# Recommendation tower on one core: the first chunk's gathers, constants and pair tiles in another order and on other engines

## The chip, the cores and the metric

One core of one Trainium2 chip. The metric is the device time of one execution in microseconds (us), lower is better. Before the change: 1389.95 us, the median of 3 runs (1387.94 to 1392.07).

## The reference, cut to what matters

For 1024 samples, 39 tables give one row of 16 numbers each, `e[b, f, d]`. Three layers follow, each a sum over all pairs of an original field and a field of the layer before, and then a small network:

```
e  = stack([tbl_f[ids[:, f]] for f in range(39)], axis=1)      # 1024 x 39 x 16
x1 = einsum('hjk,bjd,bkd->bhd', W0, e, e)  + b0                # 128 x 16 per sample
x2 = einsum('hjk,bjd,bkd->bhd', W1, e, x1) + b1
x3 = einsum('hjk,bjd,bkd->bhd', W2, e, x2) + b2
z  = concat([x1.sum(d), x2.sum(d), x3.sum(d), dense_ctx])
y  = relu(relu(z @ W_top1 + b_top1) @ W_top2 + b_top2) @ W_top3
```

## The kernel before, in words

The samples are worked in 8 chunks of 128. A step function of each engine is called for c = -1, 0, ..., 9; step c does layer 1 (`x2`) of chunk c in 16 slices d, and around it layer 0 of the next half chunk, the gathers of the chunks after, and the third layer and the network of the chunks before. In step -1 there is no layer 1: it is the start-up, and the change is in it and in the code ahead of it.

**Getting a chunk in.** GpSimd copies the chunk's indices into `idx` (L402, later L415) and issues 39 indirect DMAs (`gather`, L396 to L399), one a table, into `e_in`. ScalarE copies `e_in` into `e_mid`, the first 58 columns of `e_both`: the 39 fields, and 19 of them once more behind (L514, L515). TensorE transposes it (L900), ScalarE copies the result to `x0_t` (L555), where a field is a partition; four copies q = 0 to 3, two a half chunk. Ahead of the first gather GpSimd also makes the identity matrix (L403, L405) and clears the rest of `e_both` (L407).

**Layer 0** works on products of a field and a shifted field. A half chunk (1024 columns) has 7 pair tiles (`PAIR_TILES`); a chunk's tiles are numbered 0 to 13, so tile 7, the eighth, is the first of the second half. A tile holds 3 shifts of 39 rows, 117 partitions (the seventh 2 shifts, 78 partitions). For each, SyncE issues one DMA a shift from `x0_t` to the tile's slot (`pair_tile`, L312), 156 KB each. `x0_rep` holds the unshifted fields three times over (`rep`, L319; for the very first half ScalarE issues these three, L596). Then a tile passes through four operations: the product in place (VectorE L720 for tiles 0 to 7 of chunk 0, GpSimd L429 for all others), its upper part `pairs_hi` (ScalarE L532), its low part `pairs_lo` (VectorE L725 or GpSimd L440), and 6 matmuls into `l0_ps` (L843 to L845). The first seven tiles of chunk 0 have 4 slots, two of them in `x2_r`; all later ones have 2. `pairs_hi` and `pairs_lo` have 2 buffers.

**Order around the change.** Each engine works in the order in which its program is written; semaphores are counters. In step -1, slice d = 8 to 15 handles tile d - 8 of chunk 0 on VectorE (`first_pairs`: product and low part of the same tile, with the wait for ScalarE between them) and on ScalarE (`pair_upper`). SyncE waits before tile 4, 5 and 6 for the low part of tile 0, 1 and 2 (L306); it reloads `x0_rep` once all 7 products are made (`rep(c + 1, 1)`, L317), and loads tile 7 behind that. TensorE multiplies tile 0 to 6 in step -1; then ScalarE makes `x1_hi` (L503), VectorE `x1_lo` and a partial sum (L690, L699), and layer 1 of chunk 0 begins. There, in each slice d, TensorE does ten groups of matmuls (L938 to L940) into a ring of 4 banks; ScalarE (L626) and VectorE (L777 to L785) scale and add them. TensorE's queue takes tile 7 behind group 3 and group 5 of slice 0, tile 8 in slice 1, and so on, and waits there for the tile's low part. ScalarE makes `pairs_hi` of tile 7 ahead of its first group, and that of tiles 8 to 13 ahead of group 7 of slices 0 to 5.

GpSimd's order: 39 gathers of chunk 0; in step -1 the 24 first gathers of chunk 1 (slices 6 to 15, three of them in slice 15); in slices 0 to 4 of step 0 the product of tile 8 + d, three gathers, the low part of tile 8 + d.

```
        def tile_made(c, d, layer1, following):
            if d < PAIR_TILES - 1:
                return (c, PAIR_TILES + 1 + d) if layer1 else None
            if d < D // 2:
                return None
            return (c + 1, d - D // 2) if following else None
```

Of the kernel before, what the change touches and what calls it, by code (L numbers as in the profile page):

```python
# [4 lines left out]
FIELDS, D, H = 39, 16, 128  # L5
# [4 lines left out]
def build_tower(nc, dense_ctx, ids, tables, W_top1, b_top1, W_top2, b_top2, W_top3, W0, b0, W1, b1, W2, b2, out):  # L10
# [90 lines left out]
    Z0_AT = {1: (7, 7), 0: (15, 8)}  # L101

    MID, MOVE_MID, HI_MID, G_EARLY = 3, 2, 7, 8
    MADE_MID, LO_MID = 1, 7
    BLOCK_FIRST, BLOCK_SLOTS = 7, 4

    GATHERS = (3, 3, 3, 3, 3, 0, 6, 5, 1, 1, 2, 2, 1, 2, 1, 3)
# [9 lines left out]
    with ctx:  # L117
# [163 lines left out]
        def _(sp):  # L281
# [18 lines left out]
            def step(c, odd, layer1, following, previous, mlp, gathers):  # L300
# [68 lines left out]
                if following:  # L369
                    if layer1:  # L370
                        rep(c + 1, 0)
                    else:
                        after(sp, x0t_ready, 2)
                    for i in range(PAIR_TILES):
                        pair_tile(c + 1, i)
                        if layer1 and i in X2_WRITES:
                            x2_write(c, X2_WRITES[i])
                    rep(c + 1, 1)
                    pair_tile(c + 1, PAIR_TILES)
# [14 lines left out]
        @block.gpsimd  # L394
        def _(pool):
            def gather(chunk, f):  # L396
                nc.gpsimd.indirect_dma_start(  # L397
                    e_in[:, f, :], None, tables[f], bass.IndirectOffsetOnAxis(ap=idx[:, f:f + 1], axis=0)
                ).then_inc(gathered, 16)  # L399

            pool.wait_ge(ids_in, 16)
            nc.gpsimd.tensor_copy(idx[:, :], ids_sb[:, 0, :]).then_inc(idx_ready, 1)  # L402
            nc.gpsimd.memset(ident[:, :], 0.0).then_inc(zeroed, 1)  # L403
            pool.wait_ge(zeroed, 1)
            nc.gpsimd.affine_select(out=ident[:, :], in_=ident[:, :], compare_op=ALU.not_equal, fill=1.0, base=0,  # L405
                                    pattern=[[-1, P]], channel_multiplier=1).then_inc(consts_made, 1)
            nc.gpsimd.memset(e_both[:, WRAPPED:WRAPPED + FIELDS, :], 0.0).then_inc(e_cleared, 1)  # L407
            pool.wait_ge(idx_ready, 1)
            for f in range(FIELDS):
                gather(0, f)  # L410
# [1 line left out]
            def step(c, odd, layer1, following, previous, mlp, gathers):  # L412
# [6 lines left out]
                def multiply_pairs(chunk, i):  # L419

                    half, t = TILE[i]
                    n = TILES * chunk + i
                    rows = ROWS_OF[t]
                    products, loaded, count = pair_slot(chunk, i)
                    if isinstance(chunk, int) and chunk == 0 and i == PAIR_TILES + 1:
                        pool.wait_ge(pair_made, n)
                    after(pool, rep_in, 16 * PER_TILE * (2 * chunk + half + 1))
                    after(pool, loaded, count)
                    nc.gpsimd.tensor_tensor(products[0:rows, :], x0_rep[0:rows, :], products[0:rows, :],  # L429
                                            ALU.mult).then_inc(pair_made, 1)  # L430

                def lower_pairs(chunk, i):

                    n = TILES * chunk + i
                    rows = ROWS_OF[TILE[i][1]]
                    if isinstance(chunk, int) and chunk == 0 and i == PAIR_TILES + 1:
                        pool.wait_ge(pair_lo, n)
                    after(pool, pair_hi, n + 1)
                    after(pool, pair_used, n - 1)
                    nc.gpsimd.tensor_tensor(pairs_lo[0:rows, i % 2, :], pair_slot(chunk, i)[0][0:rows, :],  # L440
                                            pairs_hi[0:rows, i % 2, :].bitcast(f32),
                                            ALU.subtract).then_inc(pair_lo, 1)
# [11 lines left out]
                        own[:, :].unsqueeze(1).to_broadcast(shape), ALU.mult).then_inc(block_made, 1)  # L454

                for d in range(D):
                    made = tile_made(c, d, layer1, following) if layer1 else None
                    if made:
                        multiply_pairs(*made)
                    if previous and BLOCK_FIRST <= d < BLOCK_FIRST + G_GROUPS // 2:  # L460
                        for i in range(2):
                            make_block(2 * (d - BLOCK_FIRST) + i)
# [5 lines left out]
                    if gathers and d >= INDEX_SLICE:  # L468
                        for f in range(sum(GATHERS[INDEX_SLICE:d]), sum(GATHERS[INDEX_SLICE:d + 1])):
                            gather(c + 2, f)  # L470
                    if made:
                        lower_pairs(*made)

            steps(pool, step)
# [2 lines left out]
        def _(act):  # L477
# [20 lines left out]
            def step(c, odd, layer1, following, previous, mlp, gathers):  # L498
# [7 lines left out]
                def move_x0(d):  # L506

                    if following and d == MOVE_SLICE:
# [2 lines left out]
                        after(act, e_cur_ready, c + 1)  # L511
                        if layer1:
                            act.wait_ge(dve_unit, summed(c, CUR_FROM, 0))
                        nc.scalar.activation(e_mid[:, 0:FIELDS, :], e_in[:, :, :], ACT.Copy)  # L514
                        nc.scalar.activation(e_mid[:, FIELDS:WRAPPED, :], e_in[:, 0:WRAPPED - FIELDS, :],  # L515
                                             ACT.Copy).then_inc(e_mid_ready, 1)
                    if layer1 and d == COPY_SLICE:
                        after(act, dve_unit, summed(c, 0, 0))
# [68 lines left out]
                for d in range(D):  # L587
                    if not layer1:
# [4 lines left out]
                        if following and d == X0T_SLICES[0] + 1:  # L593
                            act.wait_ge(x0t_ready, 2)
                            for n in range(PER_TILE):
                                act.dma_start(x0_rep[n * FIELDS:(n + 1) * FIELDS, :],  # L596
                                              x0_t[0:FIELDS, 0:HALF]).then_inc(rep_in, 16)
                        for half, chunk in halves(c, layer1, following):
                            if d == X1_HI_AT[half][0]:
                                x1_half(chunk, half)  # L600
# [37 lines left out]
        @block.vector  # L638
        def _(dve):

            dve.wait_ge(w0_in, 16)
            nc.vector.tensor_copy(v_raw[:, 0:FIELDS], w0_raw[:, 0:FIELDS * FIELDS:FIELDS + 1])
            for s in range(1, SHIFTS):
# [41 lines left out]
            def step(c, odd, layer1, following, previous, mlp, gathers):  # L685
# [20 lines left out]

                def first_pairs(d, g):

                    made = tile_made(c, d, layer1, following)
                    made_at, lo_at = (8, 9) if d == D - 1 else (MADE_MID, LO_MID)  # L710
                    if made and g in (made_at, lo_at):
                        chunk, i = made
                        n = TILES * chunk + i
                        half, t = TILE[i]
                        rows = ROWS_OF[t]
                        products, loaded, count = pair_slot(chunk, i)
                        if g == made_at:
                            after(dve, rep_in, 16 * PER_TILE * (2 * chunk + half + 1))
                            after(dve, loaded, count)
                            nc.vector.tensor_tensor(products[0:rows, :], x0_rep[0:rows, :], products[0:rows, :],  # L720
                                                    ALU.mult).then_inc(pair_made, 1)
                        else:
                            after(dve, pair_hi, n + 1)
                            after(dve, pair_used, n - 1)
                            nc.vector.tensor_tensor(pairs_lo[0:rows, i % 2, :], products[0:rows, :],  # L725
                                                    pairs_hi[0:rows, i % 2, :].bitcast(f32),
                                                    ALU.subtract).then_inc(pair_lo, 1)

                def sum_terms(e, part):

# [16 lines left out]
                def side_work(d, g):  # L747
                    for half, chunk in halves(c, layer1, following):
                        if (d, g) == X1_LO_AT[half]:
                            x1_lower(chunk, half)  # L750
                        if (d, g) == Z0_AT[half]:
                            z0_half(chunk, half, odd)
                    if not layer1:
                        first_pairs(d, g)

                for d in range(D):
# [218 lines left out]
```

## Time and profile before

| | us |
|---|---|
| median of 3 runs | 1389.95 |
| lowest, highest | 1387.94, 1392.07 |
| the profiled execution's own time | 1388.79 |
| its span in the trace | 1386.9 |
| mean granted TensorE clock | 0.969 |
| TensorE busy | 1277.4 (92%) |
| VectorE, ScalarE, GpSimd busy | 1082.3, 1042.6, 893.5 |

How to read it: times in the trace count from the span's start; 1.9 us of the execution's time lie outside the span. A row of a timeline says when an instruction started, how long it took, its engine, its source line, out<-in, and in brackets how long its engine stood idle before it and what ended that. A letter q behind the engine is its queue issuing a DMA. TensorE's busy time is that of matmuls alone; the granted clock is a share of 2.4 GHz, so 0.5 is 1.2 GHz.

### The profile page before, as it was taken

Reading aid. Unit: us, or ns where it says so; the run is one execution under the profiler, and the core shown is the slowest. Engines: PE = TensorE matmul, PEld = TensorE weight load, DVE = VectorE, ACT = ScalarE, POOL = GpSimd, SP = SyncE. Lnnn points to the kernel's source line nnn. Section 1 sums busy time; section 2 is a strip of 40 time slices with the busy share of each in tenths; the row PEclk is TensorE's granted clock in tenths of the full one; section 3 lists DMA queues with packets and bytes.
Section 4 is the critical chain, followed back from the end, with each engine's and each line's share of the span. In section 5 each row is a group of like instructions: output and inputs, shape, how many; then the busy total and the mean of one; then the engine's idle time right before and its main releaser. Section 6 shows DMA issues by size and latency. Waiting matters only on the chain.

```text
span 1386.9 us, 23238 instructions
## 1 busy us (share of the span) xinstructions
PE 1277.4 (92%) x6029; PEld 1041.8 (75%) x6029; DVE 1082.3 (78%) x2681; ACT 1042.6 (75%) x3356; POOL 893.5 (64%) x663
## 2 busy tenths in 40 slices
PE   3179999999999999999999999999999999999986
PEld 3147777777888787887878777887878788887775
DVE  3068999988877988789877988789877988779940
ACT  2228888878877888788867888688877888688842
POOL 6658676877776687667867597667876266441111
PEclk8559999999999999999999999999999999999998
DMA  6243223413232223303242223313233123310010
GB/s 221 42 115 68 46 72 80 106 30 83 67 97 46 48 63 85 92 21 80 62 108 50 52 63 74 92 33 72 56 90 79 32 68 83 89 32 9 18 39 0
DMA packets 71116, 92.39 MB, mean 67 GB/s; under 512 B 31776, under 2 KB 53792, under 8 KB 69696
## 3 DMA queue, kind: packets, MB, share of 16 engines
q1 hardware_dynamic: 60836, 87.75, 24.4%
q0 software_dynamic: 9984, 2.58, 2.1%
q8 instruction: 53, 0.87, 0.3%
q14 instruction: 87, 0.71, 0.2%
q10 hardware_dynamic: 156, 0.48, 0.1%
HBM read 21.03 MB, written 10.95 MB: 23 GB/s over the span
## 4 chain that ended last, share of the span: by engine, by line
PE 70%; POOL 8%; DVE 7%; issue 6%; DMA 3%; ACT 2%; SPq 2%; ACTq 0%; DVEq 0%; POOLq 0%
PE ring L938 16%; PE ring L940 15%; PE ring L939 15%; PE side L856 5%; POOL e_in L397 4%; PE side L915 4%; PE l_ps L843 4%; PE l_ps L845 3%; PE l_ps L844 3%; DVE terms L785 3%; DVE x_s L741 2%; PE side L871 2%; POOL pairs L429 2%; DMA x_rep<-x_t 2%; POOL pairs_lo L440 2%
## 5 line engine op out<-in xcount | busy, mean ns | idle before, releaser
L626 ACT ACTIVATE terms<-ring,e_both 128x128 f32<-128x128 f32 x2944 | 836.3, 399 | 221.9 <-PE ring L940 219.9
L938 PE MATMUL ring<-w_hi,x_hi 128*128 128x512 f32 (+1 forms) x1280 | 544.8, 426 | 31.4 <-DVE terms L785 27.7
L785 DVE SCALAR_TENSOR_TENSOR terms<-ring,e_both,terms 128x128 f32<-128x128 f32 x1792 | 508.2, 344 | 62.7 <-PE ring L940 58.0
L940 PE MATMUL ring<-w_hi,x_lo 128*128 128x512 f32 (+1 forms) x1280 | 499.7, 390 | 0.0
L939 PE MATMUL ring<-w_lo,x_hi 128*128 128x512 f32 (+1 forms) x1280 | 498.2, 389 | 0.0
L741 DVE TENSOR_REDUCE x_s<-terms 128x32 f32<-128x800 f32 x512 | 488.9, 976 | 0.1
L440 POOL TENSOR_TENSOR pairs_lo<-pairs,pairs_hi 117x1024 fp32r<-117x1024 f32 (+1 forms) x104 | 250.2, 2406 | 191.6 <-ACT pairs_hi L532 190.6
L397 POOL DMA_INDIRECT e_in<-in_tbl,idx x312 | 306.1, 981 | 88.3 <-issue 79.4
L938 PEld LDWEIGHTS ring<-w_hi,x_hi 128*128 128x128 f32 x1280 | 242.8, 190 | 103.0 <-DVE terms L785 42.1
L429 POOL TENSOR_TENSOR pairs<-x_rep,pairs 117x1024 f32<-117x1024 f32 (+1 forms) x104 | 250.3, 2407 | 92.3 <-DMA pairs<-x_t 89.3
L939 PEld LDWEIGHTS ring<-w_lo,x_hi 128*128 128x128 f32 x1280 | 243.4, 190 | 49.2
L940 PEld LDWEIGHTS ring<-w_hi,x_lo 128*128 128x128 f32 x1280 | 241.5, 189 | 50.8
L451 POOL TENSOR_TENSOR blocks<-xb,own 128x312 f32<-128x312 f32 x128 | 90.5, 728 | 87.7 <-PE side L915 87.7
L777 DVE SCALAR_TENSOR_TENSOR terms<-ring,e_both,b_rows 128x128 f32<-128x128 f32 x128 | 44.8, 350 | 119.7 <-PE ring L940 119.5
L532 ACT ACTIVATE pairs_hi<-pairs 117x1024 fp32r<-117x1024 f32 (+1 forms) x109 | 119.7, 1099 | 19.1 <-DVE pairs L720 18.2
L843 PE MATMUL l_ps<-pairs_hi,v_hi 117*128 117x512 f32 (+1 forms) x224 | 96.4, 430 | 21.8 <-DVE pairs_lo L725 16.9
L856 PEld LDWEIGHTS side<-g_t,w_t 128*128 128x128 f32 x624 | 88.0, 190 | 12.1 <-ACT g_t L539 2.4
L845 PE MATMUL l_ps<-pairs_lo,v_hi 117*128 117x512 f32 (+1 forms) x224 | 91.8, 410 | 0.0
L844 PE MATMUL l_ps<-pairs_hi,v_lo 117*128 117x512 f32 (+1 forms) x224 | 91.7, 409 | 0.0
L856 PE MATMUL side<-g_t,w_t 128*128 128x128 f32 x624 | 89.3, 274 | 1.4 <-ACT g_t L539 1.4
L915 PE MATMUL side<-blocks,x_r 128*128 128x320 f32 x256 | 89.0, 434 | 0.9 <-issue 0.3
L843 PEld LDWEIGHTS l_ps<-pairs_hi,v_hi 117*128 117x128 f32 (+1 forms) x224 | 44.0, 196 | 39.8 <-DVE pairs_lo L725 21.2
(65 smaller groups left out, 610.6 us busy)
## 6 DMA issues: line engine op xcount, KB each, us to landing
pairs<-x_t SPq DMA_DIRECT2D x312, 156.0 KB
x_scratch<-x_s SPq DMA_DIRECT2D x32, 256.0 KB, 2.2
x_r<-x_scratch SPq DMA_DIRECT2D x8, 1024.0 KB, 6.0
x_rep<-x_t SPq DMA_DIRECT2D x45, 156.0 KB
g_t<-in_L_rec_W SPq DMA_DIRECT2D x2, 2496.0 KB, 9.5
e_in<-in_tbl,idx POOLq DMA_INDIRECT x312
x_scratch<-e_both SPq DMA_DIRECT2D x8, 312.0 KB, 7.2
xb<-x_scratch SPq DMA_DIRECT2D x8, 312.0 KB, 3.9
```

Of the source, the lines that this page charges most:

```text
L397: nc.gpsimd.indirect_dma_start(e_in[:, f, :], None, tables[f], bass.IndirectOffsetOnAxis(ap=idx[:, f:f + 1], axis=0)).then_inc(gathered, 16)
L429: nc.gpsimd.tensor_tensor(products[0:rows, :], x0_rep[0:rows, :], products[0:rows, :], ALU.mult).then_inc(pair_made, 1)
L440: nc.gpsimd.tensor_tensor(pairs_lo[0:rows, i % 2, :], pair_slot(chunk, i)[0][0:rows, :], pairs_hi[0:rows, i % 2, :].bitcast(f32), ALU.subt ...
L626: last = nc.scalar.activation(term(d, ACT_BEFORE[d][g] + i), twos(ring[:, (GROUPS * d + g) % RING, i * H:(i + 1) * H]), ACT.Copy, scale=sc ...
L741: last = nc.vector.tensor_reduce(twos(x2_s[:, d % X2_SLOTS, h]), terms[:, d % 2, a, 0:TERMS[d], :].rearrange("p a t b -> p a b t"), AX.X, ...
L785: nc.vector.scalar_tensor_tensor(out=acc, in0=y, scalar=scale_of(j, d), in1=acc, op0=ALU.mult, op1=ALU.add).then_inc(dve_unit, 1)
L843: nc.tensor.matmul(acc, v_hi[0:rows, t, :], p_hi, start=(t == 0), stop=False)
L856: last = nc.tensor.matmul(side[:, 0, 0:P], w2_t[:, j * H:(j + 1) * H], g_t[:, j, :], start=(j == 0), stop=(j == FIELDS - 1))
L915: nc.tensor.matmul(side[:, r % 2, 0:SAMPLES_PER_G * GCOLS], x2_r[:, r, :], blocks[:, r % BLOCK_SLOTS, :, :].rearrange("p b j -> p (b j)"), ...
L938: nc.tensor.matmul(acc, x1_hi[:, x], w1_hi[:, w], start=True, stop=False)
L939: nc.tensor.matmul(acc, x1_hi[:, x], w1_lo[:, w], start=False, stop=False)
L940: nc.tensor.matmul(acc, x1_lo[:, x], w1_hi[:, w], start=False, stop=True).then_inc(y_group, 1)
```

## The change

Five edits, all in what runs before layer 1 of chunk 0:

- GpSimd makes the identity matrix first and then waits for the indices; the clearing of `e_both` goes to VectorE, as its first instruction.
- The gathers of chunk 0 write `e_mid` itself; the copy L514 falls away for it, and L515 reads `e_mid`.
- The three loads of tile 1 are issued by ScalarE, behind its three of `x0_rep`, and no more by SyncE.
- VectorE makes the product of tile i + 1 before the low part of tile i.
- Tile 7 of chunk 0 is multiplied and lowered by GpSimd, ahead of the last three gathers of its step -1.

```
-    MADE_MID, LO_MID = 1, 7
+    FIRST_MADE_AT, FIRST_LO_AT, FIRST_BY_ACT = 1, 3, 1
...
                     for i in range(PAIR_TILES):
+                        if not layer1 and i == FIRST_BY_ACT:
+                            continue
                         pair_tile(c + 1, i)
...
             def gather(chunk, f):
+                dst = e_mid if isinstance(chunk, int) and chunk == 0 else e_in
                 nc.gpsimd.indirect_dma_start(
-                    e_in[:, f, :], None, tables[f], bass.IndirectOffsetOnAxis(ap=idx[:, f:f + 1], axis=0)
+                    dst[:, f, :], None, tables[f], bass.IndirectOffsetOnAxis(ap=idx[:, f:f + 1], axis=0)
                 ).then_inc(gathered, 16)
-            pool.wait_ge(ids_in, 16)
-            nc.gpsimd.tensor_copy(idx[:, :], ids_sb[:, 0, :]).then_inc(idx_ready, 1)
             nc.gpsimd.memset(ident[:, :], 0.0).then_inc(zeroed, 1)
             pool.wait_ge(zeroed, 1)
...
-            nc.gpsimd.memset(e_both[:, WRAPPED:WRAPPED + FIELDS, :], 0.0).then_inc(e_cleared, 1)
+            pool.wait_ge(ids_in, 16)
+            nc.gpsimd.tensor_copy(idx[:, :], ids_sb[:, 0, :]).then_inc(idx_ready, 1)
...
                 for d in range(D):
-                    made = tile_made(c, d, layer1, following) if layer1 else None
+                    made = tile_made(c, d, layer1, following) if layer1 or d == D - 1 else None
                     if made:
                         multiply_pairs(*made)
+                        if not layer1:
+                            lower_pairs(*made)
...
-                    if made:
+                    if made and layer1:
                         lower_pairs(*made)
...
-                        nc.scalar.activation(e_mid[:, 0:FIELDS, :], e_in[:, :, :], ACT.Copy)
-                        nc.scalar.activation(e_mid[:, FIELDS:WRAPPED, :], e_in[:, 0:WRAPPED - FIELDS, :],
+                        if layer1:
+                            nc.scalar.activation(e_mid[:, 0:FIELDS, :], e_in[:, :, :], ACT.Copy)
+                        came_in = e_in if layer1 else e_mid
+                        nc.scalar.activation(e_mid[:, FIELDS:WRAPPED, :], came_in[:, 0:WRAPPED - FIELDS, :],
                                              ACT.Copy).then_inc(e_mid_ready, 1)
...
+                            products, loaded, _ = pair_slot(0, FIRST_BY_ACT)
+                            for n in range(PER_TILE):
+                                s = PER_TILE * FIRST_BY_ACT + n
+                                act.dma_start(products[n * FIELDS:(n + 1) * FIELDS, :],
+                                              x0_t[s:s + FIELDS, 0:HALF]).then_inc(loaded, 16)
...
+            nc.vector.memset(e_both[:, WRAPPED:WRAPPED + FIELDS, :], 0.0).then_inc(e_cleared, 1)
             dve.wait_ge(w0_in, 16)
...
                 def first_pairs(d, g):
-                    made = tile_made(c, d, layer1, following)
-                    made_at, lo_at = (8, 9) if d == D - 1 else (MADE_MID, LO_MID)
...
+                    if g == FIRST_MADE_AT and tile_made(c, d, layer1, following) and d < D - 1:
+                        chunk, i = tile_made(c, d, layer1, following)
...
+                        after(dve, rep_in, 16 * PER_TILE)
+                        after(dve, loaded, count)
+                        nc.vector.tensor_tensor(products[0:rows, :], x0_rep[0:rows, :], products[0:rows, :],
+                                                ALU.mult).then_inc(pair_made, 1)
+                    if g == FIRST_LO_AT and tile_made(c, d - 1, layer1, following):
+                        chunk, i = tile_made(c, d - 1, layer1, following)
...
+                        after(dve, pair_hi, i + 1)
+                        after(dve, pair_used, i - 1)
+                        nc.vector.tensor_tensor(pairs_lo[0:rows, i % 2, :], pair_slot(chunk, i)[0][0:rows, :],
+                                                pairs_hi[0:rows, i % 2, :].bitcast(f32),
+                                                ALU.subtract).then_inc(pair_lo, 1)
```

## Rows read from the trace of the kernel before

**Rows 1.** Windows, layer 1 of chunk 0, one a slice: length, busy (x) per engine, clock, DMA

```profile
core 0: us, PE busy (x) PEld busy (x) DVE busy (x) ACT busy (x) POOL busy (x), PEclk, DMA share, GB/s
104.80:113.25 8.45, 8.38 (x37) 6.67 (x37) 5.57 (x21) 7.36 (x26) 7.67 (x6) 1.00 0.25 60
113.25:121.70 8.45, 8.45 (x38) 6.60 (x37) 7.83 (x21) 7.28 (x24) 7.66 (x6) 1.00 0.27 62
```

**Rows 2.** Chain of work that ended last, start to first loads: start, us, what

```profile
51.50 0.94 POOL e_in L397
...
52.75 2.34 DMA e_in<-in_tbl,idx
55.20 0.72 ACT e_both L514
...
61.50 7.95 DMA x_rep<-x_t
```

**Rows 3.** Timeline of GpSimd: start, us, what, idle before

```profile
3.48 0.21 POOL L402 COPY idx<-ids_sb 128x39 int32<-128x39 int32 x1 [3.03 <-DMA ids_sb<-in_ids]
...
5.10 1.15 POOL L397 DMA_INDIRECT e_in<-in_tbl,idx  x1 [0.17 <-issue]
...
90.62 1.97 POOL L397 DMA_INDIRECT e_in<-in_tbl,idx  x1 [0.30 <-issue]
92.89 0.94 POOL L397 DMA_INDIRECT e_in<-in_tbl,idx  x1 [0.30 <-issue]
104.71 2.41 POOL L429 TENSOR_TENSOR pairs<-x_rep,pairs 117x1024 f32<-117x1024 f32 x1 [10.87 <-DMA pairs<-x_t]
...
110.78 2.42 POOL L440 TENSOR_TENSOR pairs_lo<-pairs,pairs_hi 117x1024 fp32r<-117x1024 f32 x1
113.15 2.40 POOL L429 TENSOR_TENSOR pairs<-x_rep,pairs 117x1024 f32<-117x1024 f32 x1
```

**Rows 4.** Timeline of SyncE's queue: DMA issues merged (x is their count)

```profile
59.01 9.69 SPq L312 DMA_DIRECT2D pairs<-x_t  x6
68.74 7.40 SPq L312 DMA_DIRECT2D x_r<-x_t  x6
76.24 6.16 SPq L312 DMA_DIRECT2D pairs<-x_t  x6
82.50 1.54 SPq L312 DMA_DIRECT2D x_r<-x_t  x2
91.84 2.33 SPq L319 DMA_DIRECT2D x_rep<-x_t  x3
```

**Rows 5.** Windows while the loads of step -1 run, columns as in rows 1

```profile
62.90:69.50 6.60, 0.00 (x0) 0.00 (x0) 0.03 (x1) 1.07 (x2) 4.83 (x6) 0.50 0.58 132
...
76.20:84.00 7.80, 6.19 (x13) 3.98 (x14) 5.55 (x6) 2.11 (x2) 6.28 (x6) 0.50 0.58 146
...
87.70:91.80 4.10, 3.52 (x9) 2.25 (x8) 2.94 (x3) 1.06 (x1) 3.49 (x3) 0.50 0.05 4
```

**Rows 6.** Timeline of VectorE: first and last of the seven tiles, tile 7

```profile
69.47 1.23 DVE L720 TENSOR_TENSOR pairs<-x_rep,pairs 117x1024 f32<-117x1024 f32 x1 [45.01 <-DMA x_rep<-x_t]
71.82 1.25 DVE L725 TENSOR_TENSOR pairs_lo<-pairs,pairs_hi 117x1024 fp32r<-117x1024 f32 x1 [1.12 <-ACT pairs_hi L532]
73.00 1.21 DVE L720 TENSOR_TENSOR pairs<-x_rep,pairs 117x1024 f32<-117x1024 f32 x1
...
90.56 1.21 DVE L720 TENSOR_TENSOR x_r<-x_rep,x_r 78x1024 f32<-78x1024 f32 x1
...
101.15 1.22 DVE L720 TENSOR_TENSOR pairs<-x_rep,pairs 117x1024 f32<-117x1024 f32 x1 [0.42 <-DMA pairs<-x_t]
```

**Rows 7.** Timeline of ScalarE: the second copy of e_both, pairs_hi of tile 7

```profile
55.83 0.44 ACT L515 ACTIVATE e_both<-e_in 128x304 f32<-128x304 f32 x1
...
102.41 1.06 ACT L532 ACTIVATE pairs_hi<-pairs 117x1024 fp32r<-117x1024 f32 x1 [4.13 <-DVE pairs L720]
```

**Rows 8.** Timeline of TensorE: start of layer 1, tiles 7 and 8

```profile
99.75 0.76 PE L938 MATMUL ring<-w_hi,x_hi 128*128 128x512 f32 x1 [2.62 <-DVE x_lo L690]
...
104.87 0.47 PE L843 MATMUL l_ps<-pairs_hi,v_hi 117*128 117x512 f32 x1 [0.44 <-DVE pairs_lo L725]
...
113.25 0.50 PE L843 MATMUL l_ps<-pairs_hi,v_hi 117*128 117x512 f32 x1
```

**Rows 9.** Windows around a stall of TensorE in chunk 1, columns as in rows 1

```profile
277.40:280.90 3.50, 1.19 (x5) 1.02 (x6) 3.14 (x7) 0.15 (x1) 3.50 (x2) 0.99 0.02 2
280.90:284.30 3.40, 3.40 (x10) 2.62 (x9) 0.00 (x0) 2.46 (x9) 2.94 (x3) 0.50 0.38 96
```

More of the change, by code:

```diff
@@ L424, in multiply_pairs @@
                     products, loaded, count = pair_slot(chunk, i)
-                    if isinstance(chunk, int) and chunk == 0 and i == PAIR_TILES + 1:
+                    if isinstance(chunk, int) and chunk == 0 and i == PAIR_TILES:
                         pool.wait_ge(pair_made, n)
@@ L435, in lower_pairs @@
                     rows = ROWS_OF[TILE[i][1]]
-                    if isinstance(chunk, int) and chunk == 0 and i == PAIR_TILES + 1:
+                    if isinstance(chunk, int) and chunk == 0 and i == PAIR_TILES:
                         pool.wait_ge(pair_lo, n)
@@ L707, in first_pairs @@
                 def first_pairs(d, g):
-                    made = tile_made(c, d, layer1, following)
-                    made_at, lo_at = (8, 9) if d == D - 1 else (MADE_MID, LO_MID)
[L711 to L715, printed above, removed]
-                        products, loaded, count = pair_slot(chunk, i)
[L717 to L727, printed above, removed]
@@ new lines, in first_pairs @@
+                    if g == FIRST_MADE_AT and tile_made(c, d, layer1, following) and d < D - 1:
+                        chunk, i = tile_made(c, d, layer1, following)
+                        rows = ROWS_OF[TILE[i][1]]
+                        products, loaded, count = pair_slot(chunk, i)
+                        after(dve, rep_in, 16 * PER_TILE)
+                        after(dve, loaded, count)
+                        nc.vector.tensor_tensor(products[0:rows, :], x0_rep[0:rows, :], products[0:rows, :],
+                                                ALU.mult).then_inc(pair_made, 1)
@@ new lines, in first_pairs @@
+                    if g == FIRST_LO_AT and tile_made(c, d - 1, layer1, following):
+                        chunk, i = tile_made(c, d - 1, layer1, following)
+                        rows = ROWS_OF[TILE[i][1]]
+                        after(dve, pair_hi, i + 1)
[3 more added lines that the diff above has]
+                                                ALU.subtract).then_inc(pair_lo, 1)
@@ L752, in side_work @@
                             z0_half(chunk, half, odd)
-                    if not layer1:
+                    if following and not layer1:
                         first_pairs(d, g)
```

## The prediction

> **What bounds the kernel now.** I read the windows first. In layer 1 of chunk 0 TensorE is busy 8.38 and 8.45 of 8.45 us a slice [rows 1]; whatever delays the start of this stage is added to the end, since nothing later is idle enough to take it back. So the question is only when a few early marks fall. The chain of waits says what makes them: 39 gathers, one a 1.25 us, a landing, two copies, a transposition, then the load of `x0_rep`, 7.95 us [rows 2]. After that the chain goes from tile to tile. I therefore follow three marks: S, the first load out of `x0_t`, at 59.0 [rows 4]; M, the product of tile 6, at 90.56 [rows 6]; and L, the end of the low part of tile 8, at 113.2 [rows 3]. L matters because GpSimd goes straight from it to the next product [rows 3]: its slice of product, three gathers and low part lasts 113.15 - 104.71 = 8.44 us, TensorE's 113.25 - 104.87 = 8.38 [rows 8], and TensorE takes up tile 8 at 113.25, 0.05 after L. For the first slices of chunk 0 GpSimd is as much the bound as TensorE, and it has no gap in which to catch up. The shift of L is the change of the whole time.
>
> **S.** The index copy ends at 3.69, the first gather starts at 5.10 [rows 3]; between them lie only the constants. With these first, the gather follows after the 0.17 that stands before it today: 3.86, 1.24 us earlier. The identity fits into the 3.03 us in which GpSimd waits for the indices. The clearing costs VectorE nothing: it idles until its weights arrive at the start, and if that cover were gone it would be 0.6 us. The gathers keep their 1.25 us, also into `e_mid`: same rows, same sizes. Of the two copies, from 55.20 to 56.27, one of 0.44 stays [rows 2, 7]: 0.63 less. S moves by 1.87, to 57.1.
>
> **From S to M: the loads.** VectorE's new order takes out its wait for ScalarE, 1.12 of a 3.53 us cycle [rows 6]: two operations at 1.18, 2.35 us a tile. If nothing else held, M would fall 13.0 after the first product (two products, a low part, then 4 cycles of 2.35), which starts 10.45 after S: 57.1 + 10.45 + 13.0 = 80.5. But the loads don't come so fast. 23 transfers of 156 KB (3 of `x0_rep`, 20 of tiles) start at S, and traffic falls to 4 GB/s from 87.7 on [rows 5], 28.7 us later: some 1.2 us each if 1.5 are latency (my estimate). The rate is 132 GB/s while both queues issue and 146 with SyncE's alone [rows 5]: a second issuer moved no more. So ScalarE's issuing of tile 1 frees SyncE's queue, not the transfers. Tile 5 lands at about 86.1 today: the last two transfers were issued 0.77 apart [rows 4] and end at 87.7. That is S + 27.1.
>
> In-order work adds something. Tile 1 used to follow tile 0 in SyncE's queue; now tile 2 does, and tile 1 shares with it from ScalarE's. At S + 10.45 some 7.5 transfers are through, 6 of them `x0_rep` and tile 0; tiles 1 and 2 have 4.5 left and end together at S + 15.8 (bounds: S + 14 as today, where VectorE found tile 1 there at 73.00; S + 19.5 if it ends last of the 15). VectorE now stands at the product of tile 1 while the low part of tile 0 could be made, and SyncE waits for that low part before tile 4: S + 15.8 + 2.4 = S + 18.2, against S + 17.2 today [rows 4]. Of this microsecond I take half, since the engines still have tile 3 to move: tile 5 lands at S + 27.6, 84.7. Behind its product comes the low part of tile 4, and then M: 84.7 + 2.4 = 87.1, 3.4 earlier than before.
>
> **From M to L: tile 7.** Its loads stay behind M: SyncE issues at M + 1.28 [rows 4], six transfers, landed at M + 10.5 (VectorE starts at 101.15 [rows 6]). Today VectorE and ScalarE then need 3.6, and GpSimd, which is idle for 10.87 us, starts tile 8 at M + 14.15, when that has landed [rows 3]. Now GpSimd does the work itself:
>
> - product at M + 10.6, 2.41 us [rows 3], to 13.1;
> - `pairs_hi`, 1.06 [rows 7], to 14.2; low part 2.41, to 16.65;
> - three gathers that used to lie in its idle time, 3.66 (107.12 to 110.78 [rows 3]), to 20.3: the moved instructions count in full, as they are ahead of tile 8;
> - tile 8: product 2.41, gathers 3.66, low part 2.42: M + 28.8.
>
> Today L is M + 22.64. So GpSimd pays 6.15 for a start 3.4 earlier: L = 87.1 + 28.8 = 115.9 against 113.2, **2.7 us later**.
>
> TensorE's side is hidden under this. It takes tile 5 only after M + 2.4 and tiles 5 and 6 back to back, so `x1_hi` comes 1.4 later after M than now and layer 1 at M + 10.6 (today 9.2 [rows 8]). Four groups at 1.2 GHz end by M + 15.7, before tile 7 is ready at 16.65; it then needs 8.4 to tile 8, M + 25.0, and waits 3.8. ScalarE stands in that stretch at group 7 for the product of tile 8 (M + 22.7): a new wait, and the ring's banks behind it stop TensorE for some 2.4 us, inside the same 3.8. VectorE's denser work stretches more gathers to 1.97 instead of 0.94 (today some of those beside its products are [rows 3]); 21 of them still end before tile 7 has landed.
>
> **Sum.** 1.87 (S) + 1.55 (loads and VectorE) - 6.15 (GpSimd) = 2.7 slower: 1388.8 + 2.7 = 1391.5 by the profiled execution, whose time is 1.16 under the median. Against the median: 1392.6. A difference under 0.3% (4.2 us) can't be told from none, so this is "no change that can be told".
>
> **Rivals.**
>
> 1. **Issue was the bound, not the transfers.** SyncE's 20 issues last 25.0 us, 1.25 each, though the last two took 0.77 each [rows 4]; read literally, three fewer bring the later tiles 3.75 earlier: tile 5 at S + 23.4, M at 82.9, L at 111.7: 1.5 faster, 1388.4. With no load late, M is 80.5 and L 109.3: 3.9 faster, 1386.0. Against it: the equal rates of rows 5. The Trainium skill (DMA: Bandwidth & Descriptors, "Issuing engines are not separate DMA queues") also holds that issuing from several engines saves the issuing time alone; by it the sum stays as it is, and the rates agree. 0.17.
> 2. **Slower: tile 1 lands last.** If the two queues share less evenly, tile 1 comes with the fifteenth transfer, S + 19.5. Low part of tile 0 at S + 21.9; then SyncE issues tile 4, tile 5 comes some 3 us behind it and lands near S + 31, its product, tile 4's low part, then M at S + 33.5, 90.6: nothing gained there, L at 119.4, 6.2 slower, 1396.2. It decides from S + 17.5 on, where L passes 4.2 later. For it: `x0_rep`, issued by ScalarE beside SyncE's loads, took 7.95 us to land [rows 2]. 0.14.
> 3. **The clock falls.** In chunk 1 TensorE was busy 1.19 of 3.5 us and then had a granted clock of 0.5 (1.2 GHz) for 3.4 us [rows 9]. A stall like that ahead of L costs half of the next 3.4 us, 1.7: 4.4 slower, 1394.4. Here 2.4 and 1.4 us of waiting lie close together, so it can be. The Trainium skill (TensorE: Matmul & The Clock Gate, "Part 1: The HAM clock gate") has the clock follow recent activity, down after idleness and up after work; rows 9 agree. 0.12.
> 4. **GpSimd's chain is not the bound.** Should it find slack that I don't see, layer 1's start counts: 87.1 + 10.6 = 97.7 against 99.75, 2.0 faster, 1388.0. Against it: rows 3 show no idle time behind 104.71. 0.07.
>
> My forecast itself has 0.5. The range 1386.0 to 1396.5 reaches from the second price of rival 1 to rival 2. Chances: faster by over 0.3% 0.09 (only gains that no row supports), within 0.68 (forecast, rivals 1 and 4, part of the unknown rest), slower by over 0.3% 0.23 (rivals 2, 3 in the main).
>
> **What would show it.** In the trace after: first gather at 3.9; one copy of 0.44 and S at 57.1; VectorE's products of tiles 2 to 6 each waiting for `DMA pairs<-x_t`, M near 87; GpSimd's product of tile 7 near 98, three gathers before tile 8, L near 116; TensorE's matmul of tile 8 waiting for `pairs_lo`, some 1 to 4 us. Slices of 8.4 behind it, and a span 2 to 3 us longer. It is wrong if products follow one another without waits for DMA (rival 1), if VectorE's second product waits over 8 us (rival 2), or if the clock reads 0.5 behind L (rival 3). If L falls before 113 the whole argument on GpSimd fails.

## The result, and the profile after

| | before | after |
|---|---|---|
| median of 12 runs | 1389.97 us (1387.94 to 1392.07) | 1397.3 us (1391.91 to 1399.3) |
| ratio, 95% interval | | 1.0048 [1.0035, 1.006] |
| profiled execution, its span | 1388.8, 1386.9 | 1397.21, 1395.4 |
| S, first load out of `x0_t` | 59.01 | 57.35 |
| M, product of tile 6 | 90.56 | 88.80 |
| L, end of the low part of tile 8 | 113.20 | 117.49 |
| `pairs_hi` of tile 9 | 116.97 | 122.80 |

The changed kernel is 0.48% slower, outside the range. The runs after are also less alike: 7.4 us from the fastest to the slowest against 4.1, the fastest (1391.91) with a mean granted clock of 0.978, the slowest (1399.3) with 0.971. Four of the five sets of runs below were taken while every kernel, the one before too, took 37 to 52 us more, so kernels are compared within their set alone, and of their traces only distances between marks are used.

GpSimd's timeline of the changed kernel (start, us, what, idle before):

```profile
3.46 0.21 POOL L409 COPY idx<-ids_sb 128x39 int32<-128x39 int32 x1 [1.98 <-DMA ids_sb<-in_ids]
3.96 1.15 POOL L400 DMA_INDIRECT e_both<-in_tbl,idx  x1 [0.29 <-POOL idx L409]
...
99.41 2.37 POOL L431 TENSOR_TENSOR pairs<-x_rep,pairs 117x1024 f32<-117x1024 f32 x1 [14.86 <-DMA pairs<-x_t]
103.00 2.37 POOL L442 TENSOR_TENSOR pairs_lo<-pairs,pairs_hi 117x1024 fp32r<-117x1024 f32 x1 [1.22 <-issue]
105.52 0.99 POOL L400 DMA_INDIRECT e_in<-in_tbl,idx  x1 [0.15 <-issue]
106.82 0.94 POOL L400 DMA_INDIRECT e_in<-in_tbl,idx  x1 [0.30 <-issue]
108.07 0.94 POOL L400 DMA_INDIRECT e_in<-in_tbl,idx  x1 [0.30 <-issue]
109.03 2.41 POOL L431 TENSOR_TENSOR pairs<-x_rep,pairs 117x1024 f32<-117x1024 f32 x1
...
115.10 2.39 POOL L442 TENSOR_TENSOR pairs_lo<-pairs,pairs_hi 117x1024 fp32r<-117x1024 f32 x1
117.43 2.39 POOL L431 TENSOR_TENSOR pairs<-x_rep,pairs 117x1024 f32<-117x1024 f32 x1
```

Against [rows 3] the first gather is 1.14 earlier, and GpSimd starts a product 5.3 earlier (99.41 for 104.71); but it is the product of tile 7, and tile 8 begins at 109.03, 4.3 later than before, because a low part and three gathers stand between. From there to L it takes 8.46, against 8.49 before.

The timelines of SyncE's queue and of VectorE show why M gained 1.76 only, about what S did:

```profile
57.35 3.96 SPq L312 DMA_DIRECT2D pairs<-x_t  x3
61.36 12.48 SPq L312 DMA_DIRECT2D x_r<-x_t  x6
76.86 2.33 SPq L312 DMA_DIRECT2D pairs<-x_t  x3
```

```profile
68.36 1.23 DVE L727 TENSOR_TENSOR pairs<-x_rep,pairs 117x1024 f32<-117x1024 f32 x1 [42.39 <-DMA x_rep<-x_t]
74.46 1.24 DVE L727 TENSOR_TENSOR pairs<-x_rep,pairs 117x1024 f32<-117x1024 f32 x1 [4.88 <-DMA pairs<-x_t]
75.62 1.21 DVE L734 TENSOR_TENSOR pairs_lo<-pairs,pairs_hi 117x1024 fp32r<-117x1024 f32 x1
...
86.52 1.23 DVE L727 TENSOR_TENSOR pairs<-x_rep,pairs 117x1024 f32<-117x1024 f32 x1 [1.65 <-DMA pairs<-x_t]
...
88.80 1.22 DVE L727 TENSOR_TENSOR x_r<-x_rep,x_r 78x1024 f32<-78x1024 f32 x1
```

Tile 1 comes late: its product waits 4.88 us. The low part of tile 0 stands behind it and ends at 76.83; SyncE, through with tile 3 at 73.84, waits 3.0 us for it and issues tile 4 at 76.86, which was S + 17.2 before and is S + 19.5 now.

TensorE's timeline, the waits only (idle before in brackets):

```profile
98.60 0.77 PE L947 MATMUL ring<-w_hi,x_hi 128*128 128x512 f32 x1 [2.61 <-DVE x_lo L702]
105.51 0.47 PE L852 MATMUL l_ps<-pairs_hi,v_hi 117*128 117x512 f32 x1 [1.45 <-POOL pairs_lo L442]
113.62 0.50 PE L947 MATMUL ring<-w_hi,x_hi 128*128 128x512 f32 x1 [1.76 <-ACT terms L637]
117.54 0.80 PE L852 MATMUL l_ps<-pairs_hi,v_hi 117*128 117x512 f32 x1 [0.69 <-POOL pairs_lo L442]
```

From tile 7 to tile 8 it was 8.38 [rows 8] and is 12.03. The wait of 1.76 "for ACT" is GpSimd's as well: ScalarE stands at `pairs_hi` of tile 8 and waits there 2.10 us for GpSimd's product, and the ring's banks behind it stay full. The matmul at 117.54 took 0.80 for 0.50 [rows 8]: the clock. Windows of the same kernel (columns as in [rows 1]) around L, and around the stall of chunk 1:

```profile
111.40:114.80 3.40, 1.64 (x7) 1.03 (x7) 0.58 (x3) 3.33 (x11) 2.63 (x4) 1.00 0.05 5
114.80:118.20 3.40, 2.71 (x8) 1.60 (x7) 3.16 (x10) 1.73 (x7) 3.38 (x3) 0.50 0.03 2
118.20:121.60 3.40, 3.40 (x10) 2.64 (x9) 1.60 (x2) 1.09 (x4) 2.94 (x3) 0.50 0.53 130
121.60:125.00 3.40, 3.40 (x17) 2.88 (x16) 1.81 (x5) 3.27 (x10) 2.61 (x3) 0.99 0.15 23
...
282.10:285.50 3.40, 1.29 (x6) 0.71 (x4) 3.40 (x10) 1.54 (x6) 2.61 (x2) 1.00 0.04 2
285.50:288.90 3.40, 2.63 (x6) 2.15 (x7) 1.36 (x2) 0.00 (x0) 3.24 (x3) 0.50 0.27 75
288.90:292.30 3.40, 3.40 (x9) 2.64 (x9) 0.00 (x0) 2.94 (x9) 2.66 (x3) 0.50 0.17 24
```

TensorE is busy 1.64 of 3.4 us and then has 1.2 GHz for 6.8 us: in the third row ten matmuls fill 3.40 us, in the fourth row seventeen do. Before, there was no 0.5 at this place. In chunk 1 the stall of [rows 9] is there again, but is followed by 6.8 us at 0.5 instead of 3.4.

So the profiled 8.4 adds up in steps. L is 4.3 later. `pairs_hi` of tile 9 is another 1.5 later (5.31 behind L, 3.77 before), so 5.8 in all. ScalarE's `pairs_hi` of the tiles behind it are 5.7 to 6.3 later up to chunk 1's stall, and nothing takes these back; behind the stall they are 7.5 and 7.8 later, and from the next chunk on 8.0 to 8.2. ScalarE's timeline, tile 9 of before (first fence) and of after:

```profile
116.97 1.11 ACT L532 ACTIVATE pairs_hi<-pairs 117x1024 fp32r<-117x1024 f32 x1
```

```profile
122.80 1.07 ACT L538 ACTIVATE pairs_hi<-pairs 117x1024 fp32r<-117x1024 f32 x1
```

### The profile page after: what moved, and what is told of

It is laid out like the page before. It is cut to its first block, busy times and chain, and to the rows that moved or that the text cites. A ratio compares the mean times of both kernels' runs of the same rounds, so it can differ in the third digit from the quotient of the medians.

```text
span 1395.4 us, 23237 instructions
## 1 busy us (share of the span) xinstructions
PE 1276.8 (92%) x6029; PEld 1042.9 (75%) x6029; DVE 1080.6 (77%) x2680; ACT 1040.4 (75%) x3355; POOL 893.5 (64%) x664
## 4 chain that ended last, share of the span: by engine, by line
PE 70%; DVE 8%; POOL 4%; issue 4%; DMA 3%; ACT 2%; SPq 1%; DVEq 0%; ACTq 0%; POOLq 0%
PE ring L947 16%; PE ring L949 16%; PE ring L948 16%; PE side L865 5%; PE side L924 4%; PE l_ps L852 3%; PE l_ps L854 3%; PE l_ps L853 3%; DVE terms L794 3%; DVE x_s L750 3%; PE side L880 2%; POOL pairs_lo L442 2%; POOL pairs L431 1%; DMA x_rep<-x_t 1%; DMA pairs<-x_t 1%
## 5 line engine op out<-in xcount | busy, mean ns | idle before, releaser
L400 POOL DMA_INDIRECT e_in<-in_tbl,idx x273 | 265.2, 971 | 75.6 <-issue 67.6
L538 ACT ACTIVATE pairs_hi<-pairs 117x1024 fp32r<-117x1024 f32 (+1 forms) x109 | 119.7, 1098 | 17.2 <-DVE pairs L727 7.7
```

What stands on the lines that cost most here:

```text
L400: nc.gpsimd.indirect_dma_start(dst[:, f, :], None, tables[f], bass.IndirectOffsetOnAxis(ap=idx[:, f:f + 1], axis=0)).then_inc(gathered, 16)
```

## The experiments

My theory (A in the expectations): GpSimd's serial chain sets L (6 later behind M), the loads set M, and the clock falls because TensorE waits for the chain. Rivals: VectorE's new order or the late tile 1 costs the time (B), the transfers alone set M in whatever order they are issued (C), the clock costs nothing in the total (D). Sets: A (four kernels; before 1441.8), B (1389.08), C (1429.64), D (1426.63), E (1429.04).

**Tile 7 back on VectorE** (set A; again in set C as e10).

```diff
-                    made = tile_made(c, d, layer1, following) if layer1 or d == D - 1 else None
+                    made = tile_made(c, d, layer1, following) if layer1 else None
...
+                    if d == D - 1 and g in (8, 9):
...
```

> The changed kernel with one part undone: tile 7 of chunk 0 is multiplied and lowered by VectorE again, and GpSimd begins with tile 8. Theory A (GpSimd's chain of tile 7, three gathers and tile 8 sets L, the end of the low part of tile 8): M stays at 88.8 us, L falls from 117.5 to about M + 22.6 = 111.4, 1.8 before the old kernel's 113.2; total 1.8 us under the kernel before, ratio 0.999, and no granted clock of 0.5 behind L. Theory B (the late loads or the new order of VectorE make it slower): L stays at 115 or later and the time over 1393.

Measured 1436.06, ratio 0.9971 [0.9953, 0.9989]. M came at S + 30.84, L at M + 22.76, tile 9 at L + 3.76, and the clock reads 1.0 from there to 184; the 0.5 behind that is told in the last section. GpSimd's timeline of this kernel (M is 108.38):

```profile
122.66 2.41 POOL L431 TENSOR_TENSOR pairs<-x_rep,pairs 117x1024 f32<-117x1024 f32 x1 [8.01 <-DMA pairs<-x_t]
...
128.72 2.42 POOL L442 TENSOR_TENSOR pairs_lo<-pairs,pairs_hi 117x1024 fp32r<-117x1024 f32 x1
```

> Tile 7 back on VectorE and nothing else undone, once more, for a chip that agrees with the first traces. Theory A: L at 111.4, M to L 22.5, 1.8 under the kernel before, ratio 0.9987; if the late tile 1 costs time, this kernel is slower than the one that also puts tile 1 back (ratio 0.9976 there).

Measured 1425.96, 0.9983 [0.9966, 1.0001]; L at M + 22.70. One part undone returns the whole of the 6.0 between M and L.

**The three gathers ahead of tile 7** (set A).

```diff
                     if made:
-                        multiply_pairs(*made)
-                        if not layer1:
-                            lower_pairs(*made)
...
-                    if made and layer1:
+                    if made:
+                        if not layer1:
+                            multiply_pairs(*made)
                         lower_pairs(*made)
```

> The changed kernel, but GpSimd issues the last three gathers of step -1 ahead of tile 7, in the 14.9 us in which it waits for that tile. Theory A: exactly these three gathers, 3.66 us, leave the chain: L at M + 25.0 = 113.8, 0.6 after the old kernel's; without a fall of the clock the total is about 0.6 us over the kernel before (1390.6). Theory B: nothing changes but the order of gathers, L stays at 117.5 and the time near 1397.

Measured 1440.14, 0.9998 [0.9975, 1.0021]. L at M + 25.34 (M is 107.99), 3.35 of the gathers' 3.66. GpSimd's timeline:

```profile
118.82 2.38 POOL L431 TENSOR_TENSOR pairs<-x_rep,pairs 117x1024 f32<-117x1024 f32 x1 [4.53 <-DMA pairs<-x_t]
122.41 2.35 POOL L442 TENSOR_TENSOR pairs_lo<-pairs,pairs_hi 117x1024 fp32r<-117x1024 f32 x1 [1.22 <-DMA pairs<-x_t]
124.73 2.37 POOL L431 TENSOR_TENSOR pairs<-x_rep,pairs 117x1024 f32<-117x1024 f32 x1
```

Low part and next product follow one another: the moved gathers were on the path, nearly in full. The clock still read 0.5 from 125.3 to 128.7, and tile 9 came at L + 5.02.

**Tile 1 loaded by SyncE** (set A): the `continue` of `FIRST_BY_ACT` and ScalarE's three DMAs taken out.

> The changed kernel with one part undone: SyncE issues the loads of tile 1 again, between tile 0 and tile 2. Theory A (shared queues delayed tile 1 and with it the low part of tile 0 and the loads of tile 4 to 6): VectorE's second product starts at about 71.5 instead of 74.5, SyncE's wait of 3 us ahead of tile 4 goes, M falls from 88.8 to about 87, L to 115.7; total 1.8 us less than the changed kernel, still 2.5 or more over the kernel before. Theory C (the transfers alone set M, the order does not matter): M stays at 88.8 within 0.5.

Measured 1443.2, 1.0018 [0.9999, 1.0037]. The product of tile 1 began at S + 13.86 instead of S + 17.1; M at S + 31.55, but with `pairs_hi` once waiting 3.9 us for what the profile calls remote (see the last section), so this M tells nothing; L at M + 28.67, as in the changed kernel.

**Matmuls into the waits, first try** (set A): 8 and 3 in slice 1 of chunk 0's layer 1, 12 in slice 1 of chunk 1.

```diff
+                def fill(n):
+                    for _ in range(n):
+                        nc.tensor.matmul(side[:, 0, :], x1_hi[:, 0:P], w1_hi[:, 0:BANK], start=True, stop=True)
```

> The changed kernel with 23 extra matmuls of 512 columns into a bank that nothing reads at that time: 8 in chunk 0, slice 1, behind group 0, 3 ahead of tile 8 there, 12 in chunk 1 ahead of its tile 8, each set about as long as the wait of TensorE there. Theory A (a fall of the clock adds to L's delay): L stays at 117.5, the granted clock stays 1.0 behind it and behind 285, ScalarE's upper part of tile 9 is 4.4 us later than in the old kernel instead of 5.8, and chunk 1 loses nothing more, or gains 1.7 on the old kernel, which has a fall there too: total 2.7 to 4.4 over the kernel before, 1392.7 to 1394.4, and the runs lie closer together. Theory D (the clock costs nothing, since GpSimd sets the pace): times as the changed kernel or 0.5 more.

A miss: 1444.4, 1.0016 [0.9988, 1.0044]. The 12 stood at the wrong slice (TensorE's stall in chunk 1 is at tile 11, slice 4, in all twenty traces) and cost 2.8; in chunk 0 the wait ahead of tile 7 was left, and 0.5 came from 128.1 to 131.6, ahead of L (139.61); tile 9 at L + 4.02 instead of 5.3.

**Both kernels again** (set B).

> The kernel before, unchanged, for its trace on the chip of these runs. All theories: S to M 31.5, M to L 22.6.

> The changed kernel, unchanged, for its trace and time on the chip of these runs. All theories: S to M 31.4, M to L 28.7, ratio 1.003 to 1.005.

1389.27 and 1395.45, the latter 1.004 [1.0027, 1.0054]. Every mark of the changed kernel came back: S 57.39, M 88.79, L 117.48, tile 9 at 122.80, and 0.5 from 115.05 to 121.85. In chunk 1 it was 3.4 us at 0.5 this time, not 6.8, and the span 1393.8, 1.6 shorter. `pairs_hi` is 6.1 later than in the kernel before of this set ahead of the stall and 6.1 in the chunk behind it (6.6 at the end), where the first pair of traces has 6.2 and 8.0: the second 3.4 us at 0.5 cost 1.9 there.

```profile
285.70:289.10 3.40, 2.98 (x7) 2.40 (x8) 1.15 (x2) 0.01 (x1) 3.24 (x3) 0.50 0.33 87
289.10:292.50 3.40, 3.40 (x16) 2.75 (x16) 1.23 (x5) 3.40 (x11) 2.52 (x4) 1.00 0.08 12
```

**Smaller loads** (set B): tiles 4 to 6 of chunk 0 are loaded with 256 of 1024 columns, so the products of these tiles are those of other data in the rest.

```diff
+                        if isinstance(chunk, int) and chunk == 0 and 4 <= i < PAIR_TILES:
+                            sp.dma_start(products[n * FIELDS:(n + 1) * FIELDS, 0:256],
+                                         x0_t[s:s + FIELDS, 0:256]).then_inc(loaded, 16)
+                            continue
```

> The changed kernel, but the loads of tile 4, 5 and 6 of chunk 0 bring 256 of their 1024 columns, so that the products there are left wrong. Theory A (the transfers set M once VectorE no longer waits for ScalarE): the waits of VectorE for DMA ahead of the products of tile 4 and 5, 0.3 and 1.7 us, go; the products follow at 2.3 us from tile 1 on, M falls from S + 31.4 to about S + 29, and L with it, M + 28.7. Theory B (VectorE, ScalarE and TensorE hold one another, the loads do not matter): M stays at S + 31.4 within 0.5.

1392.77, one execution. VectorE's timeline shows no wait for a DMA behind tile 1, and M at S + 28.97, 2.4 earlier than with the full loads in this set; L at M + 28.66.

```profile
81.84 1.22 DVE L731 TENSOR_TENSOR pairs<-x_rep,pairs 117x1024 f32<-117x1024 f32 x1
...
84.11 1.22 DVE L731 TENSOR_TENSOR pairs<-x_rep,pairs 117x1024 f32<-117x1024 f32 x1
...
86.38 1.21 DVE L731 TENSOR_TENSOR x_r<-x_rep,x_r 78x1024 f32<-78x1024 f32 x1
```

This kernel has no extra matmuls and the whole distance to L, and it shows something else: the clock fell ahead of L (115.04) and was back long before it, and tile 9 came at L + 3.77, not 5.3. Windows, then ScalarE's timeline:

```profile
104.00:107.40 3.40, 3.40 (x10) 2.62 (x9) 0.00 (x0) 1.98 (x8) 2.78 (x4) 0.50 0.57 143
113.00:119.00 6.00, 4.45 (x20) 3.29 (x19) 4.13 (x10) 3.24 (x13) 5.54 (x4) 1.00 0.31 76
```

```profile
118.81 1.11 ACT L542 ACTIVATE pairs_hi<-pairs 117x1024 fp32r<-117x1024 f32 x1
```

**Tile 7 on VectorE and tile 1 on SyncE** (set B): the edits of the first and third experiment together. What is left of the change are the start and VectorE's order.

> The changed kernel with two parts undone: tile 7 on VectorE and the loads of tile 1 on SyncE. What is left are the constants, the gathers in place and VectorE's new order. Theory A: S to M 30 or less, since tile 1 is there 3 us earlier and SyncE does not wait ahead of tile 4; M to L 22.6; 1.9 to 3.4 us under the kernel before, ratio 0.998. Theory C (the transfers alone set M, in any order of issue): S to M 31, as with tile 1 on ScalarE, and 1.8 under the kernel before.

1385.62 (1384.35 to 1389.04), 0.9976 [0.9967, 0.9986]: faster than both kernels. VectorE's and GpSimd's timelines (S is 57.32):

```profile
70.89 1.23 DVE L718 TENSOR_TENSOR pairs<-x_rep,pairs 117x1024 f32<-117x1024 f32 x1 [1.56 <-DMA pairs<-x_t]
...
85.84 1.23 DVE L718 TENSOR_TENSOR pairs<-x_rep,pairs 117x1024 f32<-117x1024 f32 x1 [1.95 <-DMA pairs<-x_t]
...
88.12 1.22 DVE L718 TENSOR_TENSOR x_r<-x_rep,x_r 78x1024 f32<-78x1024 f32 x1
```

```profile
102.08 2.43 POOL L429 TENSOR_TENSOR pairs<-x_rep,pairs 117x1024 f32<-117x1024 f32 x1 [16.01 <-DMA pairs<-x_t]
...
108.15 2.42 POOL L440 TENSOR_TENSOR pairs_lo<-pairs,pairs_hi 117x1024 fp32r<-117x1024 f32 x1
```

All of tiles 1 to 5 wait for their load, 0.4 to 1.95 each, so M at S + 30.8 is what the loads allow; the new order gains 0.75 there against 31.55 before, 1.0 against the 31.80 of the kernel before in this set. L is 110.57, 2.6 to 2.8 earlier than before.

**The fill again, ahead of tile 7 as well** (6, 8 and 3 matmuls; set C, and set E as e15).

> The changed kernel with 17 extra matmuls of 512 columns in chunk 0, into a bank that nothing reads then: 6 ahead of tile 7, 8 in slice 1 behind group 0, 3 ahead of tile 8, which fill TensorE's waits of 1.45, 1.76 and 0.69 us. Theory A (the clock's fall adds 1.5 us behind L): L stays at 117.5, the clock is 1.0 from there on, the upper part of tile 9 comes 3.8 behind L instead of 5.3; total 1.5 us under the changed kernel, ratio to the kernel before 1.003. Theory D (the clock costs nothing): 5.3 behind L as before, ratio 1.004 to 1.005.

1431.74, 1.0013 [0.9994, 1.0031]. The clock stayed at 1.0 from tile 7 to tile 9, L at M + 28.73 and tile 9 at L + 3.77, as before the change. Windows, then ScalarE's timeline:

```profile
123.70:130.50 6.80, 6.11 (x27) 4.67 (x27) 1.85 (x7) 3.91 (x15) 6.04 (x5) 1.00 0.29 72
130.50:137.30 6.80, 6.67 (x29) 4.98 (x27) 3.71 (x12) 5.01 (x16) 6.02 (x5) 1.00 0.06 8
```

```profile
141.77 1.11 ACT L538 ACTIVATE pairs_hi<-pairs 117x1024 fp32r<-117x1024 f32 x1
```

> The kernel of e7_clock_fill_early again, in the hope of an undisturbed setup. Theory A: L at 117.5, tile 9's upper part 3.8 behind it, 1.5 less than the changed kernel, ratio 1.003. Theory D (the clock costs nothing in the total): 1.004 to 1.005.

1432.79, 1.0021 [1.0004, 1.0037]; tile 9 at L + 3.76. L itself does not move.

What these two show is less than it looks. The extra matmuls kept the clock: with all 17 of them (these two and e11) it did not fall between tile 7 and tile 9, and without them it fell in all seven traces with the same distance from M to L. But L + 3.8 is no proof that they won back 1.5 us. Of the seven, only the two of the changed kernel have the 0.5 behind L, and only these have tile 9 at L + 5.3. In the other five (e3, e5, e8, e13, e16) it ended before L or 0.1 behind it, and tile 9 came at L + 3.75 to 3.81 without any extra matmul. So the 1.5 us go with a fall that reaches past L, when GpSimd is no longer what TensorE waits for; the same fall a few us earlier cost nothing at tile 9. What decides when it comes is open.

**Tile 7 on GpSimd and nothing else** (the kernel before with the edits of GpSimd's part and of tile 7; set C, and D and E as e13 and e16).

> The kernel before with one edit of the five: tile 7 on GpSimd ahead of its last three gathers of step -1. Theory A: M stays at 90.6, L goes to M + 28.7 = 119.3, 6.1 later, and the clock's fall may add 1 to 2: total 6 to 8 us over the kernel before, ratio 1.0045 to 1.006. Theory B (the order of VectorE or the late loads are what slows the changed kernel): within 2 us of the kernel before.

> As e8_tile7_gpsimd_alone: the kernel before with tile 7 on GpSimd alone. Theory A: M 90.6, L 119.3, 6.1 later; with the clock's fall 6 to 8 over the kernel before, ratio 1.0045 to 1.006. Theory B: within 2 us of it.

> The kernel of e8_tile7_gpsimd_alone again, in the hope of an undisturbed setup. Theory A: M 90.6, L 119.3, total 6 to 8 over the kernel before, ratio 1.0045 to 1.006. Theory B: within 2 us.

Ratios 1.0027 [1.001, 1.0045], 1.0045 [1.0024, 1.0066] and 1.0035 [1.0018, 1.0053]; L at M + 28.68, 28.68 and 28.64. One part done alone gives the distance of the whole change, and makes the kernel slower each time, though in none of the three did the clock add anything at tile 9.

**The start alone** (constants and clearing first, chunk 0 gathered in place; set C, and D as e14).

> The kernel before with the two edits of the start: constants ahead of the index copy and the clearing on VectorE, gathers of chunk 0 in place. Theory A: S, M and L all 1.7 to 1.9 earlier, ratio 0.9987. Theory C2 (the landings of the gathers and not their issue set S): S less than 1 earlier, ratio 0.9995 or more.

> As e9_start_alone: the kernel before with the two edits of the start alone. Theory A: S at 57.3, L at 111.4, 1.8 earlier, ratio 0.9987. Against e6_tile7_and_tile1_back (L 110.6) it shows what the new order of VectorE brings: 0.8 or nothing.

0.9975 [0.9958, 0.9991] and 0.9987 [0.9968, 1.0007]; L at M + 22.52 and 22.55. In these sets S follows something else (below), so what the ratios measure is not S's 1.7.

**A fill in chunk 1 too** (set D): 12 matmuls in slice 5 of chunk 1, once beside the 17 of chunk 0, once in the kernel of the two parts undone.

> The changed kernel with the 17 extra matmuls of e7_clock_fill_early and 12 more in chunk 1, slice 5, ahead of its tile 12, where TensorE waits 2.8 us. Theory A: L at 117.5, tile 9's upper part 3.8 behind it, no granted clock of 0.5 between 105 and 1000; 1.5 less than the changed kernel from chunk 0, 1.7 or more from chunk 1: total 2.5 to 3.5 over the kernel before, ratio 1.002, against 1.004 for the changed kernel. Theory D (the clock costs nothing in the total): ratio 1.004.

> The kernel of e6_tile7_and_tile1_back with 12 extra matmuls in chunk 1, slice 5, ahead of tile 12. Theory A: no fall of the clock there, 1.7 us less than without them: total 5 under the kernel before, ratio 0.9965 against 0.9976. Theory D: ratio 0.9976 or a little more.

Two misses: 1.0031 [1.0004, 1.0059] and 1.0058 [1.0037, 1.008]. The 12 matmuls stood one slice too late: the stall is at tile 11 in slice 4, 2.84 us in e11 and 2.49 in e12, and they ran 8 us behind it, where they found no gap and cost 2.4 to 2.7. TensorE's timeline of e11:

```profile
311.92 0.50 PE L852 MATMUL l_ps<-pairs_hi,v_hi 117*128 117x512 f32 x1 [2.84 <-POOL pairs_lo L442]
...
320.32 2.96 PE L935 MATMUL side<-w_hi,x_hi 128*128 128x512 f32 x12
```

In e12 a wait of ScalarE put M at S + 35.3. In chunk 0 of e11 tile 9 came at L + 3.75 again. What a fill of chunk 1's stall would bring was therefore never tried.

## Why the prediction was wrong, step by step

- **The shift of L is the change of the whole time**: this step failed. L came 4.3 later, not 2.7, and nothing took it back, but the whole is 8.4 by the first traces and 6.4 in set B: the falls of the clock behind L and behind chunk 1's stall came on top.
- **S**: 57.1 forecast, 57.35 measured; first gather 3.96 for 3.86, one copy of 0.46.
- **Loads, S to M**: the mis-sized term. S + 30.0 forecast, S + 31.45 measured. Tile 1 came at S + 17.1, not 15.8, inside my bounds and just short of rival 2's 17.5; SyncE reached tile 4 at S + 19.5, not 18.2; the product of tile 5 began at S + 29.2, not 27.6. Of the forecast gain of 1.55 some 0.1 is left (31.55 to 31.45). With tile 1 on SyncE (e6), SyncE reached tile 4 at S + 17.2, the product of tile 5 began at S + 28.5 and M came at S + 30.8. By this one trace the loads themselves were 0.8 longer than my S + 30.0, and of the 2.3 by which SyncE was late 0.65 reached M; I had put its delay at 1.0 and passed on half. These 0.65 are not shown beyond doubt: with tile 1 on ScalarE and no `pairs_hi` waiting for "remote", M came at S + 30.84 to 31.67 in seven traces, the lowest as early as that of e6.
- **M to L**: right in each part. Product at M + 10.61 (10.6), low part to M + 16.57 (16.65), tile 8 at M + 20.23 (20.3), L at M + 28.69 (28.8). In all eleven traces with tile 7 on GpSimd ahead of the gathers the distance is 28.64 to 28.79, in all eight with it on VectorE (the kernel before twice) 22.40 to 22.76, and with the gathers first 25.34.
- **TensorE's waits**: I had 0.95 ahead of tile 7 (M + 15.7 to 16.65) and 3.8 ahead of tile 8, 2.4 of them at the ring; measured are 1.45, and 1.76 with 0.69.
- **Rival 3, the clock**: it fell, at the place and with nearly the price given (1.7; measured 1.53). The second failing step is that I made it an alternative of 0.12 and put nothing for it into the sum: the waits of 1.4 and 2.4 us stood in my own working, and [rows 9] had shown a fall behind such a stall. That it reached past L is not something that I could have read from them: in five of seven traces it did not. It held 6.8 us, not 3.4; since TensorE waited for GpSimd until 117.49 anyway, only the 4.1 us behind it cost, half of them 2.0 at most. In chunk 1 it held twice as long in one trace (1.9 more) and not in the other. The Trainium skill (TensorE: Matmul & The Clock Gate, "HAM oscillation — how this bites in real kernels") tells of a clock that falls over and over because each stage waits for its data; these traces agree that waits for data are what comes before a fall, but the ones here are shorter than those of the page's kernel, 1.45 and 1.76, and the fall did not come back with every stage.
- **Rival 1** fell: products waited for loads, and smaller loads alone moved M by 2.4. The Trainium skill (DMA: Bandwidth & Descriptors, "Issuing engines are not separate DMA queues") expects no bandwidth from a second issuing engine; M at S + 31.45 with two issuers and S + 30.8 with one agrees. **Rival 2** was nearly met; **rival 4** fell with L.

Sum by what was measured: 4.3 + 1.5 + 0.3, and 0 to 1.9 in chunk 1, is 6.1 to 8.0; the spans differ by 8.5 and 6.4, the medians by 7.3 and 6.4. That the clock costs its 1.5 to 3.4 in the total too is read from these marks, which stay apart to the end of the traces; no ratio shows it, as the filled kernels ran only in sets without the unfilled one. The totals of the single parts are known only from the sets that took longer: tile 7 alone 0.27 to 0.45% slower, the start alone 0.13 to 0.25% faster, the two 8.1 us apart in set D.

## What to carry to other kernels

A step moved to an idle engine takes its place in that engine's order: count all that it now stands ahead of, and put queued work that has slack (here three gathers) in front of it. Where the sum contains waits of TensorE of one or two microseconds close together, put the clock into the sum, as a term between nothing and half of the stretch at 0.5 that the same trace shows behind such waits: here it cost time behind L, where TensorE was the bound, and nothing at tile 9 where it ended before L. Only a trace of the kernel without extra matmuls in the same set tells what they win. A second queue for the second transfer of an ordered stream brought it later here (S + 17.1 for 13.6), and SyncE, which waits in order behind it, was at tile 4 2.3 later.

## What the runs showed that was not expected

- Two waits of 1.45 and 1.76 us, 6.4 us apart, were followed by 6.8 us at 1.2 GHz; in the kernel before, with 0.44 ahead of tile 7 [rows 8], by none.
- The same stall does not always bring the clock down. TensorE waits 2.1 to 2.9 us at tile 11 of chunk 1 in all twenty traces; in nine of them 3.4 us at 0.5 follow, in four 6.8, in seven none (e1, e3, e4, e10, e11, e12, e14).
- In sets A, C, D and E ScalarE stood 23 to 38 us in the setup at waits whose releaser the profile calls remote, at `w_hi`; S was 77 to 79 though the gathers ended before 54, and in some `pairs_hi` waited up to 13.1 more, which moved M by up to 8 (S + 39.64 in e14). In these sets the clock also reads 0.5 for 3 to 10 us, from 76 to 86 us behind M on, and chunk 1 begins 7 to 9 us later behind L. In set B and in the first two traces no `w_hi` or `pairs_hi` waits for "remote", and this second stretch is not there. The list of waits of e9, then that of the kernel before in set B:

```profile
ACT w_hi L481 <- remote: 34.0, 4, 10.6
```

```profile
ACT w_hi L481 <- PE ring L824: 5.3, 7, 3.5
```

  What it was is open.
